# Row numbers of two gathers put together from bytes by small DMAs, in a conditioned gated feed-forward kernel

## The reference

```python
def reference(x, itok_B_1_198, L0_cond_weights, L0_ffn_w_gate, L0_ffn_w_up, L0_ffn_w_down):
    # x (32, 32, 256), cond_weights (200, 32, 32), w_gate, w_up (256, 1024), w_down (1024, 256)
    w = L0_cond_weights[itok_B_1_198]
    y = einsum('bct,bcd->bdt', x, w)
    h = silu(einsum('bsh,hi->bsi', y, w_gate)) * einsum('bsh,hi->bsi', y, w_up)
    h = sparsify_2to4(h)          # of each 4 neighbours keep the 2 of largest magnitude
    return x + einsum('bsi,ih->bsh', h, w_down)
```

## Time and profile before

| | us |
|---|---|
| median of 3 runs | 80.29 (80.14 to 80.64) |
| the profiled execution, its own time | 80.31 |
| its span, from the first to the last instruction | 78.4 |
| TensorE busy | 73.9 (94%) |
| VectorE busy | 62.7 (80%) |
| ScalarE busy | 42.1 (54%) |
| GpSimd busy | 8.1 (10%) |

### The profile page before, as it was taken

One profiled execution on the slowest core, in us unless ns is written; L12 is line 12 of the kernel. 1 busy time (PEld: TensorE's weight loads), 2 busy tenths in 40 slices (PEclk: granted clock), 3 DMA queues, 4 the chain that ended last, 5 costly groups with the idle time before them and its releaser, 6 DMA issues.

```text
span 78.4 us, 1027 instructions
## 1 busy us (share of the span) xinstructions
PE 73.9 (94%) x362; PEld 59.6 (76%) x362; DVE 62.7 (80%) x93; ACT 42.1 (54%) x62; POOL 8.1 (10%) x17
## 2 busy tenths in 40 slices
PE   3988999999999999999999999999999999999950
PEld 1328888888888888888888888888888888888840
DVE  1006884689889999599999979999999999994460
ACT  6122773799443465699897769798380402720000
POOL 3460000000000013000804000006200000000000
PEclk9999999999999999999999999999999999999999
DMA  0726979995910005900199990003994000003333
GB/s 1 273 95 168 286 234 318 302 418 180 410 67 0 0 0 98 169 0 0 36 196 199 184 192 8 4 0 67 201 180 88 0 0 0 8 0 140 135 134 126
DMA packets 4565, 9.64 MB, mean 123 GB/s; under 512 B 560, under 2 KB 2864, under 8 KB 4304
## 3 DMA queue, kind: packets, MB, share of 16 engines
q1 hardware_dynamic: 3488, 6.16, 23.0%
q0 software_dynamic: 928, 3.28, 21.9%
q10 hardware_dynamic: 144, 0.13, 0.5%
HBM read 5.38 MB, written 1.05 MB: 82 GB/s over the span
## 4 chain that ended last, share of the span: by engine, by line
PE 94%; issue 1%; DVE 1%
PE banks L579 52%; PE banks L621 28%; PE banks L541 6%; PE banks L564 4%; PE banks L591 3%; PE banks L550 1%; DVE gate_raw L455 1%; DVE warm L458 0%
## 5 line engine op out<-in xcount | busy, mean ns | idle before, releaser
L579 PE MATMUL banks<-y_hl,up_hl 128*128 128x512 f32 x96 | 24.2, 389 | 0.0
L621 PE MATMUL banks<-h_hl,down_hl 128*128 128x512 f32 (+1 forms) x102 | 22.0, 376 | 0.0
L579 PE MATMUL banks<-y_hl,gate_hl 128*128 128x512 f32 x84 | 21.4, 390 | 0.0
L621 PEld LDWEIGHTS banks<-h_hl,down_hl 128*128 128x128 f32 x102 | 18.5, 188 | 3.6
L579 PEld LDWEIGHTS banks<-y_hl,up_hl 128*128 128x128 f32 x96 | 18.0, 188 | 3.8
L579 PEld LDWEIGHTS banks<-y_hl,gate_hl 128*128 128x128 f32 x84 | 15.7, 188 | 3.2
L264 ACT ACTIVATE silu<-banks 128x512 f32<-128x512 f32 x16 | 9.6, 597 | 11.1 <-PE banks L579 10.8
L404 DVE TENSOR_TENSOR h<-banks,silu 128x512 f32<-128x512 f32 x12 | 8.2, 687 | 3.8 <-ACT silu L264 3.7
L285 ACT ACTIVATE h_hl<-h 128x1024 fp32r<-128x1024 f32 (+1 forms) x8 | 6.7, 842 | 3.9 <-DVE h L440 3.9
L440 DVE SCALAR_TENSOR_TENSOR h<-count,h 128x512 f32<-128x512 bf16 x12 | 7.9, 685 | 0.1
L271 ACT ACTIVATE x_sb<-h 128x512 f32<-128x512 f32 x8 | 4.9, 625 | 1.7 <-DVE h L404 1.7
(11 more groups left out here) (39 smaller groups left out, 66.7 us busy)
## 6 DMA issues: line engine op xcount, KB each, us to landing
h_hl<-h POOLq DMA_DIRECT2D x4, 512.0 KB, 6.1
x_sb<-in_x SPq DMA_DIRECT2D x2, 512.0 KB, 3.7
up_raw<-in_w_up SPq DMA_DIRECT2D x4, 256.0 KB, 4.3
down_raw<-in_w_down SPq DMA_DIRECT2D x1, 1024.0 KB, 7.6
gate_raw<-in_x_t SPq DMA_DIRECT2D x1, 1024.0 KB, 5.9
down_hl<-down_raw POOLq DMA_DIRECT2D x2, 512.0 KB, 4.9
gate_raw<-in_w_gate SPq DMA_DIRECT2D x3, 256.0 KB, 4.1
out<-gate_raw SPq DMA_DIRECT2D x3, 256.0 KB, 2.3
```

The source lines that it names most:

```text
L579: last = nc.tensor.matmul(dst, w_hl[w][:, s, q, k, j], y_hl[:, m, half, k], start=i == 0, stop=i == len(terms) - 1)
L621: last = nc.tensor.matmul(bank[:, begin:end], down_hl[:, s, q, j, k * P:(k + 1) * P], h_hl[:, u, m, j, begin:end], start=(q, j, m, s) == f ...
```

## The change

The table is padded from 200 to 256 rows to a chunk, so that the row number is `c * 256 + s`. With s under 256 its lowest byte is s and the next byte c; the two upper bytes are zero. The kernel no longer adds. For each half one DMA writes byte 0 of the 128 row numbers from `cond` (one byte to a partition), issued by SP; another writes bytes 1 to 3 from `place` (three bytes to a partition), issued by ScalarE. `cond_sb`, the addition on VectorE and its semaphore go. GpSimd waits, ahead of each gather, for the two DMAs of that half. SP issues the byte of the first half where it issued the array, and that of the second half after the first gate piece. ScalarE issues both `place` DMAs ahead of its first activation in the written order.

```diff
-        cond_sb = sb("cond_sb", [P, 2 * NH], i32)
         rows_sb = sb("rows_sb", [P, NH], i32)
+        rows_bytes = rows_sb.bitcast(mybir.dt.uint8).rearrange("p (f n) -> p f n", f=NH)
...
-        cond_in = sem("cond_in")
+        cond_in = [sem(f"cond_in{i}") for i in range(NH)]
+        place_in = [sem(f"place_in{i}") for i in range(NH)]
...
-        rows_done = sem("rows_done")
...
         @block.sync
         def _(sp):
-            sp.dma_start(cond_sb[:], cond).then_inc(cond_in, 16)
+            sp.dma_start(rows_bytes[:, 0, 0:1], cond[0, 0]).then_inc(cond_in[0], 16)
 
             sp.dma_start(x_sb[:, 0:GH, :], x[0]).then_inc(x_in[0], 16)
             sp.dma_start(raw_w[0][:, 0, 0, 0:2 * P], w_gate[0, 0, 0]).then_inc(first_in[0], 16)
+            sp.dma_start(rows_bytes[:, 1, 0:1], cond[1, 0]).then_inc(cond_in[1], 16)
...
-            pool.wait_ge(rows_done, 1)
             for half in range(NH):
+                pool.wait_ge(cond_in[half], 16)
+                pool.wait_ge(place_in[half], 16)
                 nc.gpsimd.indirect_dma_start(
...
+            for half in range(NH):
+                act.dma_start(rows_bytes[:, half, 1:4], place).then_inc(place_in[half], 16)
             act.wait_ge(warm_zero, 1)
...
             nc.vector.memset(warm[:], 0.0).then_inc(warm_zero, 1)
-            dve.wait_ge(cond_in, 16)
             dve.wait_ge(blocks_marked, 1 + NB)
-            nc.vector.tensor_tensor(rows_sb[:], cond_sb[:, 0:NH], cond_sb[:, NH:2 * NH], ALU.add).then_inc(rows_done, 1)
             transpose_rows(0)
...
-    table = table.reshape(S, C, CHUNKS, D // CHUNKS).transpose(2, 0, 3, 1).reshape(CHUNKS * S, -1)
+    table = table.reshape(S, C, CHUNKS, D // CHUNKS).transpose(2, 0, 3, 1).reshape(CHUNKS, S, -1)
+    table = _np.pad(table, ((0, 0), (0, 256 - S), (0, 0))).reshape(CHUNKS * 256, -1)
...
+    cond = _np.asarray(inputs["itok_B_1_198"]).reshape(NH, B // NB // NH, NB, 1).transpose(0, 2, 1, 3)
+    cond = _np.ascontiguousarray(_np.broadcast_to(cond, (NH, NB, B // NB // NH, CHUNKS))).reshape(NH, P, 1).view(_np.uint8).transpose(0, 2, 1)[..., None]
+    place = _np.zeros((P // CHUNKS, CHUNKS, 3), _np.uint8)
+    place[:, :, 0] = _np.arange(CHUNKS)
+    place = place.reshape(P, 3)
```

More of the change, by code:

```diff
@@ L8, with adaln_ffn @@
 CHUNKS = 8
-def adaln_ffn(nc: bass.Bass, x: bass.AP, x_t: bass.AP, cond: bass.AP, table: bass.AP,
+def adaln_ffn(nc: bass.Bass, x: bass.AP, x_t: bass.AP, cond: bass.AP, place: bass.AP, table: bass.AP,
               w_gate: bass.AP, w_up: bass.AP, w_down: bass.AP, out: bass.AP):
@@ L660 @@
     S, _, D = table.shape
-    table = table.reshape(S, C, CHUNKS, D // CHUNKS).transpose(2, 0, 3, 1).reshape(CHUNKS * S, -1)
+    table = table.reshape(S, C, CHUNKS, D // CHUNKS).transpose(2, 0, 3, 1).reshape(CHUNKS, S, -1)
+    table = _np.pad(table, ((0, 0), (0, 256 - S), (0, 0))).reshape(CHUNKS * 256, -1)
     NB = P // C
     NH = 2
-    cond = _np.asarray(inputs["itok_B_1_198"]).reshape(NH, B // NB // NH, NB).transpose(2, 1, 0)
-    cond = _np.broadcast_to(cond[:, :, None], (NB, B // NB // NH, CHUNKS, NH))
-    first = _np.broadcast_to((_np.arange(CHUNKS, dtype=cond.dtype) * S)[:, None], cond.shape)
-    cond = _np.concatenate([cond, first], axis=-1).reshape(P, 2 * NH)
+    cond = _np.asarray(inputs["itok_B_1_198"]).reshape(NH, B // NB // NH, NB, 1).transpose(0, 2, 1, 3)
[3 more added lines that the diff above has]
+    place = place.reshape(P, 3)
     def columns(w):
@@ L678 @@
         "cond": cond,
+        "place": place,
         "table": table,
```

## The result

The changed kernel takes 86.26 us (median of 6; 84.66 to 86.34), the kernel before 80.24 (median of 6). The ratio of 1.0589, with an interval of 1.0516 to 1.0661, counts of the changed kernel only the two executions of 84.66 and 85.40, taken as the fast ones; the median of all six is 7.5% above. The prediction of 80.15, with a range of 79.7 to 81.0, was wrong, in sign and by far.

A forecast was written before the change was run, and what follows sets the result against it. The first gather was taken to release the mixing, followed by a fixed remainder. Rows complete at 2.55 plus 0.30 start the gather at 2.85 instead of 2.99, 0.14 earlier: from 80.29 to 80.15 us, range 79.7 to 81.0.

The forecast's parts named there:

- What bounds the kernel, and where the gain or loss would show: Start of the mixing at 6.2 us: the first gather comes last, so its shift moves the end one for one.
- The fixed remainder: From the mixing to the end: TensorE alone, untouched by the change, so its length stays the same.
- rival 2: ScalarE's start: table load stays first, `place` is issued at 2.03, gather 1.1 to 2.0 later, 81.8 us; chance 0.15.
- The landing of the small DMAs: Row-number DMAs at the start: land 1.8 us after issue, shift 0, bounds -0.1 and +0.3; rows complete at 2.55.
- GpSimd's release, 0.30, bounds 0 and 0.4: Ahead of the first gather: GpSimd starts 0.30 us after a DMA landing; 0.4 allows about 0.1 for a second wait.
- VectorE: Ahead of the first gather: dropping the addition takes 0.16 us off the line; no other work there.
- Rival 1, the two issues exclude each other: DMA issues of SP and ScalarE at 0.75 alternate: gather at 3.23, 0.24 later, 80.5 us; chance 0.30.
- Covers: Delays off the line cost nothing: table load 0.8 later under 1.9 us of cover, second gather under 7 us.
- up to 0.7: Most an earlier first gather can gain, in us, since the gate copy, done at 5.42, would then be last.

The follow-up runs named there:

- warm24: The changed kernel with 24 instead of 12 matmuls on zeros at the start (`WARM_START`): 83.09 us, ratio 1.0336 to the kernel before.
- one_wait: The changed kernel with both DMAs of each half counted on one semaphore, so GpSimd waits once per gather: 84.03, 84.16, 85.70 and 85.90 us.
- spread_one: The changed kernel with small-DMA sources 64 bytes apart, one wait per gather, and VectorE's marker wait behind its transpose: 80.47 us, ratio 1.0017 to before.
- words_move: The kernel of `words` with VectorE's wait for the markers moved behind its transpose: 80.30 us, ratio 0.9998 to the kernel before.
- words: The changed kernel, but SP copies whole row numbers, 8 bytes to a partition, in one DMA, without `place` DMAs: 80.31 us, ratio 1.0001 to before.
- spread: The changed kernel with the sources of all four small DMAs 64 bytes apart in memory, nothing else: 81.06 us, ratio 1.0085 to the kernel before.

## Why the prediction was wrong

- **What bounds the kernel, and where the gain or loss would show.** Right: the mixing started when the gather let it, and 2.76 us came through one for one.
- **The fixed remainder.** Wrong, and the dearest omission, 3.2 us. I called the time "the start of the mixing plus a fixed remainder" and priced every delay one for one, rival 2 too, though that rival meant a pause of over 1.6 us for TensorE. The trace of before has no row of a longer pause; a bound for the clock was owed with every delay priced. `warm24` shows the sum for the profiled execution.
- **The landing of the small DMAs.** The term that failed first: "size hardly counts at this end of the scale", shift 0, bounds -0.1 and +0.3. Measured were 3.8 for the byte and 4.0 for `place`, against an assumed 1.8 for each. The row numbers were complete at 4.79 instead of 2.55, and this term alone puts the sum at 80.15 + 2.24 = 82.4, outside the range. Size in fact does not count; how the sources lie in memory does, and in the change their distance went from 16 bytes to 1 and 3. The rows that I used (16 bytes apart, and 1 KB a partition) lie on the flat side of the table above.
- **GpSimd's release, 0.30, bounds 0 and 0.4.** The 0.30 is right behind a DMA landing if there is one wait (0.28 in `one_wait`). With two it is 0.88, beyond my bound: I allowed 0.1 for a wait instruction and had no row for it, and the gather's own instruction starts 0.86 behind it.
- **VectorE.** I wrote that it has no other work there and gave it no price. With the addition gone, the marker wait and the gather wait meet ahead of the transpose, one becomes an instruction (DVEq L376), and the transpose starts 0.09 behind SP's issue at 8.40, where both began at 5.72 before. Moved, in `spread_one` and `words_move`, the two start together again.
- **Rival 1, the two issues exclude each other.** They did not: ScalarE issued two DMAs from 0.76 to 1.65 while SP issued two. The Trainium skill, page "Perfetto Trace Analysis", section "DMA Instruction — HWDGE (DVE, Sync)", has the generator locked for one issue at a time; in this trace no such wait shows. A slowdown beside ScalarE's packed DMA exists (2.5 to 3.3 for the byte), but in the landing.
- **Rival 2, the table load first.** It did not happen; the load is at 1.68, behind both issues, as the Trainium skill has it (page "ScalarE: Activation LUTs", section "Step-by-step: what each stage is for"). Its premise was the right worry in another form: whatever makes `place` late by over a microsecond costs far more than that.
- **Covers.** The table load's delay (0.93, forecast 0.8) was hidden, as forecast. The "up to 0.7" of possible gain was too much: the matmuls on zeros cap it. The row "1.20 4.46" already has them end at 5.66, which leaves 0.57, and over the executions profiled they end at 5.5 to 6.5. Nor was the gate piece as safe as said: it was copied at 6.51 instead of 5.00; x, too, landed 4.9 after its issue, behind the slow reads, and 3.5 before.

## What to carry to other kernels

A DMA of tiny pieces is priced by how its sources lie in memory: send whole values in one DMA as `words` does, or pad the sources to 16 bytes apart or more, and never read packed single bytes where someone waits. Before adding a second wait ahead of an instruction, let both producers count on one semaphore and wait for the sum of both, or put the idle wait behind the urgent one. And where TensorE is kept busy only to hold its clock, price each delay twice: the delay itself, and the stretch at half clock that may follow once the pause grows.

## What was not expected

- 128 reads of one byte took 2.5 us packed, 1.6 at 16 bytes apart and 1.5 to 1.7 at 64, at no difference between 1 and 4 bytes a piece. The writes were free of it, also off a word boundary (1.9 and 2.0 against 2.0).
- Behind the slow small reads x landed 1.4 us later (4.9 against 3.5 after its issue); with the sources spread it took 3.5 to 3.9.
- A separate wait instruction ahead of GpSimd's indirect DMA puts 0.86 us between them, against 0.28 to 0.30 from the release when the wait is the DMA's own.
- A pause of TensorE of 2.8 us was followed by 0.50 of the clock, and so was one of 1.9 in `one_wait` (6.50 to 8.37), where the clock fell only when the mixing was under way; in the profile of `spread` one of 0.65 us left it at 1.00. The view of stretches shows 1.00 also for the first 4 us, where the weight loads of the matmuls on zeros start 0.43 apart, against 0.21 for the same matmuls later (14 in 2.94 us in `warm24`): the column alone does not show that they run at half the pace.
